# Attention in pairs of steps: four 32-row products side by side, exponential and maximum over two PSUM banks, and one bank for the rotation solver

## The chip, the cores and the metric

One core of one Trainium2 chip. The metric is the device time of one execution in microseconds (us), as the median of several runs; a profiled execution gives the trace from which the rows below are read. The engines are named as the profile names them: PE is TensorE (matmul; PEld its weight loads), DVE is VectorE, ACT is ScalarE, POOL is GpSimd, SP is SyncE.

## The reference

The input is x of shape (2, 512, 144) and a condition vector per batch element. Three transformer layers follow one another, then a learned rotation:

```python
mod = silu(c) @ w_adaln + b_adaln                   # six vectors per batch element
h   = modulate(layernorm(x), shift, scale)
q, k, v = split(h @ w_qkv + b_qkv)                  # 16 heads of 9 columns
attn = softmax(q @ k.T * 9 ** -0.5)                 # 512 x 512 per head and batch element
x = x + gate * (attn @ v @ w_proj + b_proj)
x = x + gate2 * mlp(modulate(layernorm(x), ...))    # layer 0: 4 experts, top 2; layers 1, 2: one MLP of 576
...
R = expm(A(cond))                                   # A skew-symmetric, 64 x 64, one per batch element
```

Layer 1 also normalises each head's q and k. At the end every token is turned in the 64-dimensional subspace that the columns of P span (Q from an orthogonalisation of P, R as above). All is in float32.

## The kernel before

**Blocks, groups, steps.** There are six blocks (three layers by two batch elements). A block has 16 heads in four groups of four. A group has 16 steps (`GSTEPS`), one for each of four tiles of 128 keys and each of four heads `j`. The whole attention is 384 steps, n = 0 to 383. In a step TensorE forms the scores of one key tile and one head against all 512 queries: a product with only 32 rows of contraction (27 used), with `k_t` as weights and `q_t` moving, into one PSUM bank. Head j sits on rows 32j to 32j+31, so products of different heads use different row strips of the array. ScalarE takes the exponential of the bank into `probs` (L667). After every four steps `pv` (L1280) multiplies four heads' `probs` with `v_aug` in eight instructions, each on a strip of 32 columns, into `o_bank`.

**The row maxima.** Softmax needs each query's maximum before the scores of its group. So during group g the kernel also forms, for group g+1, the transposed products (`max_scores`, L1259; 16 per group) in `m_bank`, and VectorE reduces each of them to one column (`take_max`, L823). `MAX_SHARE` puts two of them into each of the first two steps of a group, one into each of the next twelve and none into the last two. In step 14 (`TURN_AT`) `max_turn` (L1267) transposes the maxima with four matmuls, and `place_max` (L830, VectorE) puts them into `q_t`, where they act as one more row of the contraction. The next group's scores wait for that.

**Woven work.** Everything else (adaLN vectors, norms, qkv, projections, gates, MLPs) is cut into slots and spread over the steps by `SLOTS`; it uses two `d_banks`. The solver for the rotation is three chains of small parts spread by `SOLVER_PLAN`: `mgs` and `lu` (64 each, a part every 2.5 steps, up to about step 296), and, from step 141, `skew`, `scale`, eleven `taylor`, `turned` and sixteen `square` (a part every four steps). A solver part is a small TensorE product into PSUM (L1437, L1449, L1460) followed by a chain of small VectorE operations, of which the last (`drain`) releases the bank. The next part of the same chain waits for this release.

**Banks.** Of the eight banks two are for scores, one is `o_bank`, two are for woven work, and three (`m_banks`) form one ring (class `Banks`) that maxima, turns and solver parts take in program order: whoever takes a bank waits until its previous user has drained it. A score product waits for the exponential of two steps before.

**Order on each engine.** Every engine's program is written out by one loop, and each engine runs it in order. TensorE in step n: maxima, scores, the turn of the outputs (`o_turn`), `pv`, `max_turn`, slots, solver parts. VectorE in step n: outputs, slots of step n-1, solver parts of step n-1, then maxima of step n. One of these maxima may be pulled forward (`fill_once`) into the pause of a chain of dependent operations.

```python
            def take(r):
                bk, drained, before = r.take()
                if before:
                    pe.wait_ge(drained, before)
                return bk, (drained, before + 1)
```

## Time and profile before

| | |
|---|---|
| median of 3 runs | 1083.63 us (1082.55 to 1086.33) |
| the profiled execution | 1077.8 us, of which span 1075.7 us |
| mean granted TensorE clock | 0.624 of 2.4 GHz |
| busy: PE, DVE, ACT, POOL | 857.7, 662.4, 385.2, 163.9 us |

The span runs from the first to the last instruction; the rest of an execution's time (2.1 us) lies around it. In rows of the timeline the columns are start in us, duration in us, engine, line, operation, output<-inputs, shapes and count; in brackets stands the idle time just before, with what released the engine. A busy TensorE is not one at its peak: products on different strips run at the same time and count once.

### The profile page before, as it was taken

How to read it: one execution, taken by the hardware profiler on the slowest of the kernel's cores; microseconds unless marked ns; L12 is line 12 of the kernel's file. 1: busy time of each engine (PE TensorE's matmuls, PEld its weight loads, DVE VectorE, ACT ScalarE, POOL GpSimd, SP SyncE). 2: the span in 40 equal slices, each digit the busy share in tenths (PEclk: the TensorE clock that was granted, in tenths of full speed). 3: DMA queues.
4: the chain of work that ended last, by engine and by line, in shares of the span. 5: the costliest groups of instructions: out<-in, count | busy, mean ns of one | idle time of the engine just before them, and what ended most of it. 6: DMA issues, size and time to landing. Idle time of an engine off the chain costs nothing.

```text
span 1075.7 us, 11316 instructions
## 1 busy us (share of the span) xinstructions
PE 857.7 (80%) x3551; PEld 454.5 (42%) x3551; DVE 662.4 (62%) x2080; ACT 385.2 (36%) x682; POOL 163.9 (15%) x353
## 2 busy tenths in 40 slices
PE   5565889896997679799777897979886879979856
PEld 1332333333673333477444343635333544335425
DVE  4478876777537887752578667475767364674232
ACT  0311343332451433345334331325332445545412
POOL 5201013101131000223311003011002021002020
PEclk9855665555796655569865555755555775568557
DMA  3000001000021000002200000000000000000000
GB/s 100 22 1 5 17 12 43 2 16 0 21 64 32 1 0 1 1 16 56 56 0 1 1 1 15 13 1 1 1 1 1 28 1 1 0 1 1 1 11 12
DMA packets 18108, 14.95 MB, mean 14 GB/s; under 512 B 3295, under 2 KB 15479, under 8 KB 18050
## 3 DMA queue, kind: packets, MB, share of 16 engines
q1 hardware_dynamic: 18002, 14.22, 4.8%
q8 instruction: 29, 0.48, 0.2%
q14 instruction: 29, 0.24, 0.1%
q10 hardware_dynamic: 48, 0.02, 0.0%
HBM read 13.62 MB, written 0.61 MB: 13 GB/s over the span
## 4 chain that ended last, share of the span: by engine, by line
PE 61%; DVE 31%; issue 4%; ACT 2%; POOL 2%; DMA 0%; SPq 0%; DVEq 0%; POOLq 0%; ACTq 0%
PE m_bank L1259 11%; PE o_bank L1280 11%; DVE row_max L823 8%; PE d_bank L1399 5%; PE s_bank L1248 3%; PE m_bank L1437 3%; PE d_bank L1341 3%; PE m_bank L1267 2%; PE d_bank L1385 2%; PE d_bank L1230 2%; PE d_bank L1312 2%; DVE h_tok L882 2%; PE d_bank L1386 2%; PE d_bank L1387 2%; PE d_bank L1388 1%
## 5 line engine op out<-in xcount | busy, mean ns | idle before, releaser
L667 ACT ACTIVATE probs<-s_bank 128x512 f32<-128x512 f32 x384 | 220.4, 595 | 486.1 <-PE s_bank L1248 483.5
L823 DVE TENSOR_REDUCE row_max<-m_bank 128x1 fp32r<-128x512 f32 x384 | 256.0, 686 | 151.0 <-PE m_bank L1259 145.8
L1259 PE MATMUL m_bank<-k_t,q_t 32*128 32x512 f32 x384 | 211.8, 731 | 63.1 <-DVE q_rows L1070 24.5
L1248 PE MATMUL s_bank<-q_t,k_t 32*128 32x512 f32 x384 | 233.9, 729 | 6.2 <-ACT probs L667 5.4
L1280 PE MATMUL o_bank<-probs,v_aug 128*32 128x512 f32 x768 | 172.2, 986 | 3.9 <-DVE o_tok L841 3.2
L1259 PEld LDWEIGHTS m_bank<-k_t,q_t 32*128 32x128 f32 x384 | 79.8, 264 | 181.6 <-issue 62.7
L1248 PEld LDWEIGHTS s_bank<-q_t,k_t 32*128 32x128 f32 x384 | 88.2, 265 | 30.6 <-ACT probs L667 15.6
L593 POOL TENSOR_TENSOR h_tok<-h_tok,mod 128x144 f32<-128x144 f32 x48 | 24.0, 500 | 269.2 <-DVE h_tok L882 269.2
L1399 PE MATMUL d_bank<-w_all,g_act 128*128 128x144 f32 x480 | 61.0, 287 | 0.0
L1399 PEld LDWEIGHTS d_bank<-w_all,g_act 128*128 128x128 f32 x480 | 59.4, 190 | 2.3 <-issue 2.3
L1437 PE MATMUL m_bank<-q_rows,ident 64*64 64x144 f32 x128 | 43.9, 442 | 18.9 <-DVE q_rows L1070 18.9
L1312 PE MATMUL d_bank<-ident,h_tok 128*128 128x128 f32 x80 | 32.7, 415 | 19.3 <-POOL h_tok L597 19.3
L1267 PEld LDWEIGHTS m_bank<-ident_r,row_max 128*128 128x128 f32 x96 | 21.5, 312 | 62.2 <-issue 39.2
L596 POOL COPY h_tok<-o_tok 128x144 f32<-128x144 f32 x24 | 7.4, 307 | 257.1 <-DVE o_tok L841 215.4
L733 ACT ACTIVATE g_act<-d_bank 128x512 f32<-128x512 f32 (+1 forms) x60 | 35.7, 597 | 30.0 <-PE d_bank L1388 30.0
L611 POOL TENSOR_TENSOR qs_tok<-qkv_tok,qs_tok 128x144 fp32r<-128x144 f32 x24 | 12.2, 506 | 224.6 <-ACT ks_tok L716 224.6
L1267 PE MATMUL m_bank<-ident_r,row_max 128*128 128x128 f32 x96 | 25.7, 417 | 25.7 <-DVE q_rows L1070 8.7
L1437 PE MATMUL m_bank<-lu,ident 64*64 64x64 f32 x128 | 28.2, 318 | 20.5 <-DVE lu L1092 19.1
L830 DVE SCALAR_TENSOR_TENSOR q_t<-m_bank,q_t 128x512 fp32r<-128x512 f32 x24 | 16.6, 691 | 42.7 <-PE m_bank L1267 42.7
L1437 PEld LDWEIGHTS m_bank<-lu,ident 64*64 64x64 f32 x128 | 17.1, 188 | 54.5 <-DVE lu L1092 26.0
L1437 PEld LDWEIGHTS m_bank<-q_rows,ident 64*64 64x64 f32 x128 | 17.3, 191 | 49.4 <-DVE q_rows L1070 29.5
L1341 PE MATMUL d_bank<-ident_r,qs_tok 128*128 128x128 f32 x96 | 25.1, 410 | 16.2 <-POOL ks_tok L613 16.1
(224 smaller groups left out, 1335.0 us busy)
## 6 DMA issues: line engine op xcount, KB each, us to landing
raw_a<-in_L_cond_w_dram SPq DMA_DIRECT2D x10, 288.0 KB
w_all<-in_L_cond_w_dram SPq DMA_DIRECT2D x10, 288.0 KB
w_rows<-in_L_cond_W_dram SPq DMA_DIRECT2D x8, 141.8 KB
raw_d<-in_L_cond_w_dram SPq DMA_DIRECT2D x30, 36.0 KB
x_tok<-in_x_dram SPq DMA_DIRECT2D x2, 288.0 KB, 4.5
raw_a<-in_L_cond_W_fc_dram SPq DMA_DIRECT2D x2, 288.0 KB
w_all<-in_L_cond_W_fc_dram SPq DMA_DIRECT2D x2, 288.0 KB
out_dram<-moe SPq DMA_DIRECT2D x4, 144.0 KB, 1.9
```

What stands on the lines that cost most here:

```text
L593: link(pool.tensor_tensor(tile, tile, mv[:, first + 1, :], ALU.mult))
L667: act.activation(probs[:, n % PROBS, :], s_banks[n % S_BANKS][:, :], ACT.Exp, scale=HD ** -0.5)\
L733: act.activation(g_act[0:rows, f, :], bk[0:rows, :], ACT.Gelu_apprx_tanh).then_inc(drained, 1)
L823: dve.tensor_reduce(row_max[:, grp % 2, t, MAXROW + 32 * j:MAXROW + 32 * j + 1], bk[:, :], AX.X, ALU.max).then_inc(drained, 1)
L1248: pe.matmul(s_banks[n % S_BANKS][:, :], k_t[rows, par, g, kt * P:(kt + 1) * P], q_t[rows, par, g, :], start=True, stop=True).then_inc(s["s ...
L1259: pe.matmul(bk[:, :], q_t[rows, par, g, t * P:(t + 1) * P], k_t[rows, par, g, :], start=True, stop=True).then_inc(s["max_full"], 1)
L1267: ins = pe.matmul(bk[:, t * P:(t + 1) * P], row_max[:, grp % 2, t, :], ident_r[:, :], start=True, stop=True)
L1280: ins = pe.matmul(o_bank[32 * j:32 * j + 32, :], v_aug[:, par, kt, at:at + 32], probs[:, (GRP * quad + j) % PROBS, :], start=(kt == 0), st ...
L1312: pe.transpose(a_bank[:, cols], h_tok[:, t, 0:P], ident[:, :])
L1341: ins = pe.matmul(bk[:, g * P:(g + 1) * P], src[:, g * GRP:(g + 1) * GRP, :].rearrange("p h w -> p (h w)"), ident_r[:, :], start=True, sto ...
L1399: ins = pe.matmul(dst, g_act[:, f, t * P:(t + 1) * P], w2_all[:, i, f, :], start=(f == 0), stop=(f == FT))
L1437: ins = pe.matmul(bk[0:S, 0:src.shape[1]], ident[0:S, j:j + 1].to_broadcast([S, S]), src, start=True, stop=True)
```

## The change

Two consecutive steps become one pair, 192 in all (`PAIRS`), eight to a group (`GPAIRS`). The score banks become one tensor of two banks, `s_pair`; two of the three maxima banks become `m_pair`; the third, `x_bank`, serves the solver and the turns alone, as a ring of one.

- `scores(p)` issues two products (two heads) into `s_pair` with one signal, and waits for the exponential of pair p-1. ScalarE takes the exponential over both banks with one instruction.
- `max_scores` issues two products into `m_pair` with one signal, after the scores of the pair, and waits until the previous pair of maxima is reduced (`maxed`). VectorE reduces both banks with one instruction, to two columns. For group 0, ahead of the loop, `m_pair` and `s_pair` alternate, and the wait is for the reduction two pairs before.
- `MAX_AT` gives the maxima of a pair the two heads that its scores don't use, so that four strips are in use; one extra pair of maxima comes at the end of pair 1 (after `pv`), and pair 7 has none.
- `max_turn` moves from step 14 to after the scores and `pv` of pair 7, the last. It waits for all the maxima and for `x_bank`.
- `pv` comes in odd pairs, slots and solver parts of both steps come at the end of the pair. Where both steps have a solver part, or a step has two, they follow each other on the one `x_bank`. On VectorE `fill_once` is allowed only while fewer than two such parts are left.

```diff
-S_BANKS, M_BANKS, D_BANKS = 2, 3, 2
+D_BANKS = 2
+PAIR = 2
...
-MAX_SHARE = [2, 2] + [1] * (GSTEPS - 4) + [0, 0]
-TURN_AT = GSTEPS - 2
+MAX_AT = [[(0, 1)], [(1, 0), (0, 0)]] + [[divmod(p + 1, 2)] for p in range(2, GPAIRS - 1)] + [[]]
+TURN_AT = GPAIRS - 1
...
+def slots_of(p):
+    return SLOTS[PAIR * p] + SLOTS[PAIR * p + 1]
+
+
+def parts_of(p):
+    return SOLVER_PLAN[PAIR * p] + SOLVER_PLAN[PAIR * p + 1]
...
-        s_banks = [bank(f"s_bank{i}") for i in range(S_BANKS)]
+        s_pair = ctx.enter_context(nc.psum_tensor("s_pair", [P, PAIR * 512], F32))
+        m_pair = ctx.enter_context(nc.psum_tensor("m_pair", [P, PAIR * 512], F32))
         o_bank = bank("o_bank")
-        m_banks = [bank(f"m_bank{i}") for i in range(M_BANKS)]
+        x_bank = bank("x_bank")
...
-        def ring_m():
-            return Banks(m_banks, m_drained)
+        def ring_x():
+            return Banks([x_bank], [x_drained])
...
-                act.wait_ge(s["scores_full"], n + 1)
-                act.activation(probs[:, n % PROBS, :], s_banks[n % S_BANKS][:, :], ACT.Exp, scale=HD ** -0.5)\
+                act.wait_ge(s["scores_full"], p + 1)
+                act.activation(probs[:, n % PROBS:n % PROBS + PAIR, :],
+                               s_pair[:, :].rearrange("p (i n) -> p i n", i=PAIR), ACT.Exp, scale=HD ** -0.5)\
                     .then_inc(s["probs_ready"], 1)
...
-            def take_max(grp, t, j):
-                bk, drained, _ = mring.take()
+            def take_max(grp, t, half, pair):
                 dve.wait_ge(s["max_full"], seen.next("max_full"))
-                dve.tensor_reduce(row_max[:, grp % 2, t, MAXROW + 32 * j:MAXROW + 32 * j + 1], bk[:, :], AX.X, ALU.max).then_inc(drained, 1)
+                rows = row_max[:, grp % 2, t, :].rearrange("p (j w) -> p j w", j=GRP)
+                dve.tensor_reduce(rows[:, PAIR * half:PAIR * half + PAIR, MAXROW],
+                                  pair[:, :].rearrange("p (i n) -> p i n", i=PAIR), AX.X, ALU.max)\
+                    .then_inc(s["maxed"], 1)
...
-                    taken = [mring.take() if part[0] in SOLVER_BANK else None for part in SOLVER_PLAN[n - 1]]
-                    fill[0] = fill_once
-                    for _ in range(SLOTS[n - 1]):
+                    left = sum(part[0] in SOLVER_BANK for part in parts_of(p - 1))
+                    fill[0] = fill_once if left < 2 else lambda: None
+                    for _ in range(slots_of(p - 1)):
                         next(woven)
...
+                if p:
+                    pe.wait_ge(s["probs_ready"], p)
+                for i in range(PAIR):
+                    rows = slice(32 * (first + i), 32 * (first + i) + 32)
+                    ins = pe.matmul(s_pair[:, 512 * i:512 * i + 512], k_t[rows, par, g, kt * P:(kt + 1) * P],
+                                    q_t[rows, par, g, :], start=True, stop=True)
+                ins.then_inc(s["scores_full"], 1)
...
-                bk, _ = take(mring)
-                pe.matmul(bk[:, :], q_t[rows, par, g, t * P:(t + 1) * P], k_t[rows, par, g, :],
-                          start=True, stop=True).then_inc(s["max_full"], 1)
+                if issued >= depth:
+                    pe.wait_ge(s["maxed"], issued + 1 - depth)
+                for i in range(PAIR):
+                    rows = slice(32 * (PAIR * half + i), 32 * (PAIR * half + i) + 32)
+                    ins = pe.matmul(pair[:, 512 * i:512 * i + 512], q_t[rows, par, g, t * P:(t + 1) * P],
+                                    k_t[rows, par, g, :], start=True, stop=True)
+                ins.then_inc(s["max_full"], 1)
...
-            for n in range(BLOCKS * STEPS):
-                grp = n // GSTEPS
-                if grp + 1 < BLOCKS * G:
-                    for t, j in max_tiles(n):
-                        max_scores(grp + 1, t, j)
-                scores(n)
-                if n % GSTEPS == 4 and grp > 0:
+            for p in range(PAIRS):
+                grp = p // GPAIRS
+                maxima = list(max_pairs(p)) if grp + 1 < BLOCKS * G else []
+                scores(p)
+                for t, half in maxima[:1]:
+                    max_scores(grp + 1, t, half, m_pair, 1)
+                if p % GPAIRS == 2 and grp > 0:
                     o_turn(grp - 1)
-                if n % GRP == 2 and n > GRP:
-                    pv(n // GRP - 1)
-                if n % GSTEPS == TURN_AT and grp + 1 < BLOCKS * G:
+                if p % 2 == 1 and p > 2:
+                    pv(p // 2 - 1)
+                for t, half in maxima[1:]:
+                    max_scores(grp + 1, t, half, m_pair, 1)
+                if p % GPAIRS == TURN_AT and grp + 1 < BLOCKS * G:
                     max_turn(grp + 1)
-                for _ in range(SLOTS[n]):
+                for _ in range(slots_of(p)):
                     next(woven)
-                for part in SOLVER_PLAN[n]:
+                for part in parts_of(p):
                     solver(part)
```

## Rows read from the trace of the kernel before

**Rows 1.** The cores' spans and granted clock, and the page's busy times.

```profile
core 0: 1075.7 us, clock 0.624
...
PE 857.7 (80%) x3551; PEld 454.5 (42%) x3551; DVE 662.4 (62%) x2080; ACT 385.2 (36%) x682; POOL 163.9 (15%) x353
```

**Rows 2.** The page's chain that ended last, by line.

```profile
PE m_bank L1259 11%; PE o_bank L1280 11%; DVE row_max L823 8%; PE d_bank L1399 5%; PE s_bank L1248 3%; PE m_bank L1437 3%; PE d_bank L1341 3%; PE m_bank L1267 2%; PE d_bank L1385 2%; PE d_bank L1230 2%; PE d_bank L1312 2%; DVE h_tok L882 2%; PE d_bank L1386 2%; PE d_bank L1387 2%; PE d_bank L1388 1%
```

**Rows 3.** Groups by line: count | busy, mean ns | idle before and releaser.

```profile
L667 ACT ACTIVATE probs<-s_bank 128x512 f32<-128x512 f32 x384 | 220.4, 595 | 486.1 <-PE s_bank L1248 483.5
L823 DVE TENSOR_REDUCE row_max<-m_bank 128x1 fp32r<-128x512 f32 x384 | 256.0, 686 | 151.0 <-PE m_bank L1259 145.8
...
L936 DVE TENSOR_TENSOR x_tok<-x_tok,gated 128x288 f32<-128x288 f32 x20 | 9.2, 458 | 0.7
...
L1002 DVE TENSOR_TENSOR moe<-moe,mod 128x576 f32<-128x576 f32 x2 | 1.5, 757 | 0.1
```

**Rows 4.** Windows: start:end, length, busy of PE, PEld, DVE, ACT, POOL, clock, DMA.

```profile
194.77:221.15 26.38, 22.76 (x84) 7.99 (x85) 20.40 (x67) 9.61 (x17) 0.00 (x0) 0.50 0.01 1
...
591.96:621.60 29.64, 25.02 (x104) 10.30 (x100) 18.19 (x53) 9.82 (x17) 0.00 (x0) 0.50 0.00 1
...
715.94:759.67 43.73, 40.04 (x174) 23.74 (x171) 24.76 (x68) 20.98 (x43) 4.48 (x8) 0.54 0.00 1
759.67:790.60 30.93, 26.30 (x120) 12.02 (x116) 22.09 (x61) 9.82 (x17) 0.00 (x0) 0.50 0.00 1
...
906.44:926.27 19.83, 19.16 (x76) 6.67 (x72) 11.19 (x19) 9.51 (x17) 0.00 (x0) 0.50 0.00 1
```

**Rows 5.** The same windows, PE instructions that read k_t alone (both products).

```profile
715.94:759.67 43.73, 11.01 (x32) 0.54 0.00 1
...
sum 1075.70, PE 257.98; mean PE 10.32
```

**Rows 6.** Timeline of group 19, from its first scores on.

```profile
908.34 0.79 PE L1248 MATMUL s_bank<-q_t,k_t 32*128 32x512 f32 x1
...
910.60 1.94 PE L1280 MATMUL o_bank<-probs,v_aug 128*32 128x512 f32 x8
912.47 0.28 PEld L1259 LDWEIGHTS m_bank<-k_t,q_t 32*128 32x128 f32 x1 [1.67 <-issue]
...
913.30 1.29 DVE L823 TENSOR_REDUCE row_max<-m_bank 128x1 fp32r<-128x512 f32 x2 [1.79 <-PE m_bank L1259]
913.33 1.08 ACT L667 ACTIVATE probs<-s_bank 128x512 f32<-128x512 f32 x2
...
915.24 1.94 PE L1280 MATMUL o_bank<-probs,v_aug 128*32 128x512 f32 x8
...
918.61 0.28 PEld L1248 LDWEIGHTS s_bank<-q_t,k_t 32*128 32x128 f32 x1 [1.01 <-ACT probs L667]
...
924.41 1.94 PE L1280 MATMUL o_bank<-probs,v_aug 128*32 128x512 f32 x8
926.27 0.93 PEld L1267 LDWEIGHTS m_bank<-ident_r,row_max 128*128 128x128 f32 x4 [1.66 <-issue]
```

**Rows 7.** Timeline: lu parts and what follows them, in groups 11 and 12.

```profile
603.39 0.79 PE L1259 MATMUL m_bank<-k_t,q_t 32*128 32x512 f32 x1
...
604.12 0.69 PE L1449 MATMUL m_bank<-rot,skew_b 64*64 64x64 f32 x4
...
608.23 0.47 PE L1437 MATMUL m_bank<-lu,ident 64*64 64x64 f32 x2
...
608.74 0.15 DVE L1083 TENSOR_SCALAR s_sign<-m_bank 64x1 f32<-64x1 f32 x1 [1.51 <-PE m_bank L1437]
...
623.55 0.15 DVE L1083 TENSOR_SCALAR s_sign<-m_bank 64x1 f32<-64x1 f32 x1
...
624.80 0.29 PEld L1437 LDWEIGHTS m_bank<-lu,ident 64*64 64x64 f32 x2 [0.87 <-DVE lu L1092]
```

**Rows 8.** Timeline of group 17: TensorE held by an lu part.

```profile
866.88 0.44 PE L1437 MATMUL m_bank<-lu,ident 64*64 64x64 f32 x2 [5.23 <-DVE lu L1092]
```

More of the change, by code:

```diff
@@ L739, in solver @@
                 if step[0] in SOLVER_BANK:
-                    bk, drained, before = mring.take()
+                    bk, drained, before = xring.take()
                     full = seen.next("solver_full")
@@ L1167, in solve @@
             def solve(part):
-                solver(part, mring.take() if part[0] in SOLVER_BANK else None)
+                solver(part, xring.take() if part[0] in SOLVER_BANK else None)
             for slot, _ in enumerate(side(HEAD)):
@@ L1172, in _ @@
                     solve(part)
[L1173 to L1175 removed]
+            for i in range(HALVES * T):
+                take_max(0, *divmod(i, HALVES), (m_pair, s_pair)[i % 2])
+                for part in first_parts(2 * i + 1):
                     solve(part)
```

119 lines of the change are left out of this document (56 added, 63 removed).

## The prediction

> **What bounds the kernel now.** I read the cores row first: a span of 1075.7 us at a mean granted clock of 0.624, so TensorE runs mostly at the lower of its two levels [rows 1]. The busy times name it as the fullest engine (857.7 us), VectorE next (662.4) [rows 1]. The chain by line shows that no single line bounds the time: the two kinds of 32-row products hold 14% of it, `pv` 11%, the reductions 8%, and the rest is woven work and solver parts in small shares [rows 2]. ScalarE idles 486 us before its exponentials [rows 3], so they cost nothing by their number. What counts is the order in which the in-order TensorE meets the answers of the others. So I cut the span at each turn of the maxima (L1267) into 24 windows; window k holds group k. Those without slots are short: 19.8 us without a solver (group 19), 26.4 with `mgs` (3), 29.6 with `lu` and `taylor` (11), 30.9 with `lu` and `square` (15); with six slots and a solver 43.7 (14) [rows 4]. I walk the new order through these kinds with the durations of the trace, and multiply.
>
> **Part 1, products side by side.** Products on different strips already start together: at 912.47 four of them, for two steps, are over when the first output turn begins [rows 6]. A batch with a switch of shape before and after it takes 603.39 to 604.12, so 0.73 us, at the low clock [rows 7]. Before, one step's two products make such a batch wherever a slot, a solver part or `pv` comes between two steps; after, only every pair does. TensorE is busy with these products for 258.0 us in all, 10.3 per window, 11.0 in group 14 [rows 5]. After: eight batches of 0.79 and one more of 0.43 for the extra maxima of pair 1, which use the same strips as the scores of pair 2: 6.8 us. The upper bound of the gain is 3.5 us per window. Groups with slots, where TensorE has no other reason to stop, get most of it at the low clock and about half of it at the high one. Over the 15 groups with many slots (0 to 2, 4 to 6, 8 to 10, 12 to 14, 16 to 18) I take 3.0 us in the seven that also hold solver parts of two chains (8 to 10, 12 to 14, 16), and 1.75 in the other eight, of which some wait for VectorE anyway: -21 and -14, together -35 us.
>
> **Part 2, one instruction over two banks.** The trace has none. Bounds for VectorE: two reductions in a row take 1.29 us [rows 6], so no more than that; from 288 to 576 columns an operation grows by 299 ns, 1.04 ns per column [rows 3], so 686 + 512 x 1.04 ns = 1.22. I take 1.22: 0.07 less per pair, 13 us of VectorE in all, of which perhaps a tenth is on the path (8% of the chain is this line [rows 2]): -1 us, mostly ahead of the loop, where eight rounds are paced by VectorE. For the exponentials 1.08 (two in a row [rows 6]) is the upper end; I take 1.05. The Trainium skill (Advanced Engine Details and Errata, in its part on the SBUF/PSUM latency) advises just this, several PSUM banks read by one instruction, since the latency is exposed between instructions; the 0.07 us is what this trace leaves for it, because neighbours already overlap.
>
> **Part 3, the buffers are one deep.** Scores of pair p wait for the exponential of p-1. From the issue of a batch to the start of its exponential 0.86 us pass (912.47 to 913.33), of its reduction 0.83 (to 913.30) [rows 6]; the release costs 0.05. So scores can follow each other every 0.86 + 1.05 + 0.05 = 1.96 us, and maxima every 0.83 + 1.22 + 0.05 = 2.10, at the low clock. From one `pv`'s end (912.47) to the next `pv` 2.77 us pass now with an output turn between (to 915.24) [rows 6]; after: 2.10 + 0.73 = 2.83. Equal. Two places differ. First, pair 1: after its `pv` come the extra maxima; those of pair 2 wait 2.10 us for them, with the output turn queued behind, and those of pair 3 again 2.10 for those. Group 19, from its first scores at 908.34: `pv` starts at 2.83 (now 2.26), its end is 4.7; maxima of pair 2 at 6.8, output turn 7.5 to 8.6, maxima of pair 3 at 8.9, second `pv` at 9.6 (now 6.9), third at 14.3, last at 18.8 (now 16.07, 924.41), its end is 20.6 (now 17.93, 926.27) [rows 6]. That is +2.7 us. The turn and the placing (908.34 - 906.44 = 1.9) stay. I book 2.7 for 19, 2.3 for 20 (half at the high clock), 2 for 21 to 23 together (some slots; the last has no maxima): +7. Beside this walk a rule of the Trainium skill (Perfetto Trace Analysis, Optimizing Tensor Performance, Matmuls) asks that independent products rotate through banks, so that one is emptied while the next is filled; the change takes this rotation away, and the walk is what it costs by the rows.
>
> **Part 4, the solver on one bank.** In 24 pairs two solver parts follow each other (one in each of groups 2, 8 and 16, two in 9, three in 10, 11, 13, 14 and 15, four in 12: so many by `parts_of`). Before, `taylor` or `square` went out right behind `lu` into another bank. Now it waits until `lu` is drained: 0.51 us from its issue to VectorE's first operation (608.23 to 608.74), 1.25 from there to the next product that waited for the chain (623.55 to 624.80), less the 0.40 that `lu` itself takes: 1.4 us [rows 7]. Behind it in TensorE's queue stand the next pair's scores, and ScalarE waits for those. That is the lower bound, with VectorE idle; the upper is a VectorE in the midst of a norm, which now holds TensorE 5.23 us at one `lu` [rows 8]. For the 17 in groups with slots I take 1.75: +30 us.
>
> Group 11 pair by pair, with each `lu`'s chain stretched by the reduction put into its pause (1.13): pair 0 5.45 us (products, 2.2 for the previous group's `lu`, which now stands behind the turn, `lu`, 1.4, `taylor` 0.7), pair 1 3.0, pair 2 6.4, pair 3 3.0, pair 4 5.5, pair 5 3.0, pair 6 3.55, pair 7 with turn, placing and its `lu` 4.85: 34.7 against 29.6 [rows 4], +5. Group 15 the same way, with `square`'s eight products (1.1): 37.4 against 30.9 [rows 4], +6.5. Together +11.5.
>
> Groups 3 and 7 have one part per pair, of 2.2 us on VectorE without and 2.9 with the reduction, at distances of two, two, two and four steps in place of two and three: 1.9 + 4.2 + 4.4 + 3.7 + 3.7 + 2.6 + 1.9 + 5.1 = 27.5 against 26.4 [rows 4]: +1.1 each, +2. In the eight slot groups of part 1 without a second chain the same crowding and the part that now stands behind the placing (0.4 to 0.7) make +7.
>
> **The sum.** -35 - 1 + 7 + 30 + 11.5 + 2 + 7 = +21.5 us on the profiled execution's 1077.8, so 1099.3. The median of the runs shown is 1083.63, 5.8 above that execution; I put the change on the median: 1105 us. POOL, SP and the DMAs lose nothing: their loops only drop counting. A measurement of this kernel can't tell less than 0.3% (3 us) from no change.
>
> **Rivals.** *The wait is only moved (faster).* TensorE waits for the solver today as well: 5.23 us at one `lu` [rows 8], 0.87 at another [rows 7]. If the wait at the second part only takes the place of one that came a batch or two later, the 24 pairs cost nothing: -30, and -1.4 x 6 in groups 11 and 15. Sum: 21.5 - 38.5 = -17, so 1067. The point that decides: with these pairs free the sum is -17, so they tip it when they cost 17 us, 0.73 each over the 23 that I booked. For it: such waits are in most solver groups. Against: group 11 has only 4.6 us of TensorE idle to give [rows 4], and the clock is low there either way.
>
> *VectorE falls behind (slower still).* TensorE may now lead VectorE by one pair of maxima and one solver part, where three banks let it lead by more. If each of the 20 norms costs 1.5 us more of the kind of the 5.23 [rows 8], the time is 1105 + 30 = 1135. For it: VectorE is busy 24.8 of 43.7 us in group 14 and idle in bits [rows 4]. Against: in those stretches it was VectorE's chain that set the pace already.
>
> *No effect.* Gain and loss cancel: 1081 to 1087.
>
> **How the numbers follow.** The forecast case, 1090 to 1122 (each of the two large terms off by half), 0.50; the wait only moved 0.25; VectorE behind 0.19; no effect 0.06. The likeliest is 1105. The range from 1070 to 1136 leaves out part of the first rival and the far end of the second. Faster 0.25, same 0.06, slower 0.69.
>
> **What the new profile would show.** Right: TensorE's busy time for these products near 258 - 23 x 3.5 = 178 us; the exponential near 1.05 and the reduction near 1.22 us; new idle of TensorE before L1449 and L1460 put down to `lu`; a group 19 of 22.5 us and a group 11 of 34 to 35. Wrong: idle before `taylor` and `square` small, a group 11 under 31 us, or slot groups shorter by more than 3.5 us each, which would mean that a batch costs more around itself than 0.73 us.

## The result: slower by 49 us, and the profile after

The changed kernel takes 1132.98 us (median of four runs, 1131.26 to 1135.42) beside 1084.02 us for the kernel before (four runs, 1082.55 to 1086.33): a ratio of 1.045, 95% interval 1.042 to 1.048. The forecast was slower, 1105 us. The direction was right and the time lies inside the range given, but the rise is 49 us where the sum had 21.5. The profiled execution is 55.4 us longer in span than the one before. Single executions of the kernel before lie between 1066 and 1091 us, with medians of 1084 to 1086; where they fall into shorter and longer ones, a ratio given with an interval compares the shorter ones alone.

The page of the kernel after, busy time by engine (to be set beside [rows 1]) and the chain by line (beside [rows 2]):

```profile
PE 799.3 (71%) x3551; PEld 435.4 (38%) x3551; DVE 655.5 (58%) x1888; ACT 361.1 (32%) x490; POOL 163.5 (14%) x353
...
PE 54%; DVE 34%; ACT 5%; issue 5%; POOL 2%; DMA 0%; DVEq 0%; SPq 0%; ACTq 0%; POOLq 0%
PE o_bank L1300 11%; DVE row_max L833 10%; PE s_pair L1264 9%; PE d_bank L1419 5%; PE x_bank L1457 4%; PE d_bank L1361 3%; PE m_pair L1279 3%; ACT probs L680 2%; PE x_bank L1287 2%; PE d_bank L1244 2%; PE d_bank L1405 2%; DVE h_tok L894 2%; PE x_bank L1480 1%; DVE q_rows L1082 1%; PE d_bank L1247 1%
```

TensorE lost 58 us of busy time, as it was meant to, and the kernel became longer. So TensorE's idle time grew from 1075.7 - 857.7 = 218.0 us to 1131.1 - 799.3 = 331.8: by 114. The rest of this text asks what the 114 are.

Groups by line (columns as in [rows 3]: busy and mean ns, then idle before with its releaser):

```profile
L680 ACT ACTIVATE probs<-s_pair 128x1024 f32<-128x1024 f32 x192 | 196.3, 1022 | 510.7 <-PE s_pair L1264 510.3
L833 DVE TENSOR_REDUCE row_max<-m_pair 128x2 fp32r<-128x1024 f32 x188 | 229.9, 1223 | 108.6 <-PE m_pair L1279 106.6
...
L1264 PE MATMUL s_pair<-q_t,k_t 32*128 32x512 f32 x384 | 142.2, 737 | 28.1 <-ACT probs L680 21.5
```

The two new instructions take 1022 and 1223 ns. The exponential's idle time before it grew from 486 to 511 us: ScalarE is not the engine that is short.

The waits of TensorE (engine, what waited, for what; us in total, times, longest):

```profile
PE x_bank L1457 <- DVE q_rows L1082: 63.1, 31, 6.3
PE x_bank L1457 <- DVE lu L1104: 44.6, 20, 6.6
PE x_bank L1480 <- DVE lu L1104: 31.9, 15, 5.8
PE x_bank L1469 <- DVE lu L1104: 30.3, 10, 7.3
PE s_pair L1264 <- ACT probs L680: 21.5, 21, 2.2
```

L1457 is the product of a `mgs` or `lu` part, L1480 that of `square`, L1469 that of `taylor`. These four solver rows hold 170 us of idle. The second two, 62.2 us in 25 waits, are the ones that the prediction named: a part of the second chain behind `lu`. The same waits before, and with them those of the maxima, which shared the ring with the solver:

```profile
PE m_bank L1437 <- DVE lu L1092: 19.1, 10, 5.5
PE m_bank L1437 <- DVE q_rows L1070: 18.9, 19, 2.4
PE m_bank L1449 <- DVE lu L1092: 5.0, 3, 3.7
PE m_bank L1460 <- DVE lu L1092: 2.3, 2, 1.2
PE m_bank L1259 <- DVE q_rows L1070: 24.5, 11, 7.1
PE m_bank L1259 <- DVE lu L1092: 16.9, 12, 4.1
```

They are 45.3 us for the solver's own products and 41.4 for the maxima, 86.7 in all. So 83 of the 114 us stand in front of solver products now. Where the waiting stands is not yet its cause; that takes the experiments.

The windows of groups 3, 11, 14, 15 and 19 (columns as in [rows 4], which has the same groups of before), and under them the products that read `k_t` in group 14 and in all windows (beside [rows 5]):

```profile
198.45:226.19 27.74, 21.40 (x84) 7.29 (x85) 19.79 (x59) 8.78 (x9) 0.00 (x0) 0.50 0.01 1
613.56:647.62 34.06, 22.06 (x104) 9.12 (x100) 17.69 (x45) 8.78 (x9) 0.00 (x0) 0.50 0.00 1
754.45:803.41 48.96, 36.82 (x175) 22.92 (x171) 24.19 (x60) 20.09 (x35) 4.02 (x8) 0.53 0.00 1
803.41:838.76 35.35, 24.42 (x121) 11.07 (x117) 21.55 (x53) 8.78 (x9) 0.00 (x0) 0.50 0.00 0
956.63:979.85 23.22, 18.43 (x77) 6.31 (x73) 10.97 (x11) 8.78 (x9) 0.00 (x0) 0.50 0.00 1
...
754.45:803.41 48.96, 6.90 (x32) 0.53 0.00 1
...
sum 1131.10, PE 183.84; mean PE 7.35
```

Group 14 is the plain case. Its products fell from 11.0 to 6.9 us, its TensorE time from 40.0 to 36.8, and it takes 49.0 us in place of 43.7. All of the difference is TensorE standing still: 3.7 us before, 12.1 after.

Cut at the turns of the maxima as in the prediction, and put into its classes, the 24 groups and the head (time up to the first turn) differ by:

| groups | forecast, us | measured, us |
|---|---|---|
| 8 to 10, 12 to 14, 16: slots and two chains | -21 + 30 = +9 | +37.6 |
| 0 to 2, 4 to 6, 17, 18: slots, at most one chain or few doubled pairs | -14 + 7 = -7 | +0.6 |
| 11 and 15 | +11.5 | +8.8 |
| 3 and 7 | +2 | +1.4 |
| 19 and 20 | +5 | +7.7 |
| 21 to 23 | +2 | -2.5 |
| head | -1 | +1.7 |

The miss has one place: the seven groups with slots and two chains hold 28.6 of the 34 us between the profiled difference and the sum. There the pair kernel stands like this (timeline in group 12, all engines; in brackets the idle time before an instruction):

```profile
682.67 1.02 ACT L680 ACTIVATE probs<-s_pair 128x1024 f32<-128x1024 f32 x1 [5.66 <-PE s_pair L1264]
...
684.72 0.94 DVE L875 BATCH_NORM_STATS2 stat<-x_tok 128x6 f32<-128x144 f32 x4
...
684.83 0.44 PE L1457 MATMUL x_bank<-lu,ident 64*64 64x64 f32 x2 [2.25 <-DVE lu L1104]
...
688.29 1.62 DVE L894 TENSOR_SCALAR h_tok<-x_tok,mean_var,rstd 128x144 f32<-128x144 f32 x4
...
689.83 0.14 DVE L1095 TENSOR_SCALAR s_sign<-x_bank 64x1 f32<-64x1 f32 x1
...
690.67 0.28 DVE L1104 SCALAR_TENSOR_TENSOR lu<-x_bank,s_small,lu 64x64 f32<-64x64 f32 x1
...
691.00 1.11 PE L1480 MATMUL x_bank<-rot 64*64 64x64 f32 x8 [5.73 <-DVE lu L1104]
...
692.88 1.02 ACT L680 ACTIVATE probs<-s_pair 128x1024 f32<-128x1024 f32 x1 [9.19 <-PE s_pair L1264]
```

TensorE issues the `lu` product at 684.83. VectorE is in a norm (L875 to L894) until it turns to the bank at 689.83, and it drains the bank only at 690.95. The `square` product needs that same bank, so TensorE stands for 5.73 us; the next scores are behind it in the queue, and ScalarE has nothing for 9.19 us. This is the prediction's upper case, at one place. The doubled pair in group 11, where VectorE is free, is its lower case:

```profile
618.96 0.44 PE L1457 MATMUL x_bank<-lu,ident 64*64 64x64 f32 x2 [2.08 <-DVE lu L1104]
619.51 0.15 DVE L1095 TENSOR_SCALAR s_sign<-x_bank 64x1 f32<-64x1 f32 x1 [0.70 <-PE x_bank L1457]
...
620.36 0.28 DVE L1104 SCALAR_TENSOR_TENSOR lu<-x_bank,s_small,lu 64x64 f32<-64x64 f32 x1
620.70 0.69 PE L1469 MATMUL x_bank<-rot,skew_b 64*64 64x64 f32 x4 [1.30 <-DVE lu L1104]
```

1.30 us, where the walk had 1.4. If seventeen such pairs were the cause of the 28.6 us, each would have to cost 1.75 + 1.7 = 3.4 us. That was the first theory to test.

### The profile page after: what moved, and what is told of

Read it like the earlier page. It is cut to its first block, busy times and chain, and to the rows that moved or that the text cites. A ratio compares the mean times of both kernels' runs of the same rounds, so it can differ in the third digit from the quotient of the medians.

```text
span 1131.1 us, 10906 instructions
## 1 busy us (share of the span) xinstructions
PE 799.3 (71%) x3551; PEld 435.4 (38%) x3551; DVE 655.5 (58%) x1888; ACT 361.1 (32%) x490; POOL 163.5 (14%) x353
## 4 chain that ended last, share of the span: by engine, by line
PE 54%; DVE 34%; ACT 5%; issue 5%; POOL 2%; DMA 0%; DVEq 0%; SPq 0%; ACTq 0%; POOLq 0%
PE o_bank L1300 11%; DVE row_max L833 10%; PE s_pair L1264 9%; PE d_bank L1419 5%; PE x_bank L1457 4%; PE d_bank L1361 3%; PE m_pair L1279 3%; ACT probs L680 2%; PE x_bank L1287 2%; PE d_bank L1244 2%; PE d_bank L1405 2%; DVE h_tok L894 2%; PE x_bank L1480 1%; DVE q_rows L1082 1%; PE d_bank L1247 1%
## 5 line engine op out<-in xcount | busy, mean ns | idle before, releaser
L680 ACT ACTIVATE probs<-s_pair 128x1024 f32<-128x1024 f32 x192 | 196.3, 1022 | 510.7 <-PE s_pair L1264 510.3
L833 DVE TENSOR_REDUCE row_max<-m_pair 128x2 fp32r<-128x1024 f32 x188 | 229.9, 1223 | 108.6 <-PE m_pair L1279 106.6
L1264 PE MATMUL s_pair<-q_t,k_t 32*128 32x512 f32 x384 | 142.2, 737 | 28.1 <-ACT probs L680 21.5
L1279 PE MATMUL m_pair<-k_t,q_t 32*128 32x512 f32 x376 | 140.6, 744 | 10.8 <-DVE row_max L833 10.2
L1457 PE MATMUL x_bank<-q_rows,ident 64*64 64x144 f32 x128 | 44.4, 446 | 68.6 <-DVE q_rows L1082 63.1
L1264 PEld LDWEIGHTS s_pair<-q_t,k_t 32*128 32x128 f32 x384 | 52.0, 267 | 94.2 <-ACT probs L680 53.9
L1279 PEld LDWEIGHTS m_pair<-k_t,q_t 32*128 32x128 f32 x376 | 50.9, 266 | 57.2 <-DVE row_max L833 54.9
L1457 PE MATMUL x_bank<-lu,ident 64*64 64x64 f32 x128 | 27.6, 313 | 54.9 <-DVE lu L1104 44.6
L1457 PEld LDWEIGHTS x_bank<-q_rows,ident 64*64 64x64 f32 x128 | 17.6, 194 | 96.0 <-DVE q_rows L1082 82.6
L1457 PEld LDWEIGHTS x_bank<-lu,ident 64*64 64x64 f32 x128 | 16.9, 186 | 83.2 <-DVE lu L1104 54.5
L747 ACT ACTIVATE g_act<-d_bank 128x512 f32<-128x512 f32 (+1 forms) x60 | 35.3, 595 | 32.0 <-PE d_bank L1408 31.5
L1287 PEld LDWEIGHTS x_bank<-ident_r,row_max 128*128 128x128 f32 x96 | 21.8, 316 | 51.4 <-issue 48.3
L1405 PE MATMUL d_bank<-h_hi,ff_hi 128*128 128x512 f32 x60 | 30.9, 515 | 12.7 <-ACT g_act L747 7.7
```

The costliest lines, as they stand in the source:

```text
L680: act.activation(probs[:, n % PROBS:n % PROBS + PAIR, :], s_pair[:, :].rearrange("p (i n) -> p i n", i=PAIR), ACT.Exp, scale=HD ** -0.5)\
L747: act.activation(g_act[0:rows, f, :], bk[0:rows, :], ACT.Gelu_apprx_tanh).then_inc(drained, 1)
L833: dve.tensor_reduce(rows[:, PAIR * half:PAIR * half + PAIR, MAXROW], pair[:, :].rearrange("p (i n) -> p i n", i=PAIR), AX.X, ALU.max)\
L1264: ins = pe.matmul(s_pair[:, 512 * i:512 * i + 512], k_t[rows, par, g, kt * P:(kt + 1) * P], q_t[rows, par, g, :], start=True, stop=True)
L1279: ins = pe.matmul(pair[:, 512 * i:512 * i + 512], q_t[rows, par, g, t * P:(t + 1) * P], k_t[rows, par, g, :], start=True, stop=True)
L1287: ins = pe.matmul(bk[:, t * P:(t + 1) * P], row_max[:, grp % 2, t, :], ident_r[:, :], start=True, stop=True)
```

## The experiments

The theory at the start (**solver**): the doubled pairs on one bank cost far more than 1.75 us. The rival (**order**): they cost what was booked, and it is the -35 us of the products side by side that doesn't come, since TensorE meets other waits with the time saved. Given the spread of single executions, differences under some 10 us between two variants carry little. The recorded expectations name runs by label: e4, e5 and e6 are 3, 4 and 5 here, e12 and e13 are 9 and 10, e14 and e15 are 16 and 17, e17 is 11. Their theory A is the solver theory, their rivals B and C are crowding of the solver's parts and the one-deep buffers.

**1 and 2. Without the second chain, in pairs and in steps.** The same edit in both kernels:

```diff
-EXP_CHAIN = [("skew",), ("scale",)] + [("taylor", n) for n in range(TAYLOR - 1, 0, -1)] + [("turned",)]
-EXP_CHAIN += [("square", i) for i in range(SQUARINGS)]
+EXP_CHAIN = [("skew",), ("scale",), ("turned",)]
...
-                    pe.wait_ge(*last[chain])
+                    pe.wait_ge(s["rot_ready"], 1)
```

> The pair kernel without the 11 taylor and 16 square parts (the matrix exponential is left out, so the rotation is not the reference's). This leaves 2 pairs with two parts for the one bank in place of 24. Theory A, one bank: TensorE's idle before the second parts (30.3 us before taylor, 31.9 before square) goes, and with it 22 us of small products: 1133 to about 1050, and less than 1.5% above the kernel before with the same parts left out. Rival B, crowding and one-deep buffers everywhere: only the parts' own work goes, some 25 us, and the pair kernel stays 40 us behind the kernel before with the same parts left out.

> The kernel before without the 11 taylor and 16 square parts (the matrix exponential is left out). It gives what these parts cost where they have banks to themselves: both theories say 20 to 30 us, so about 1058. The distance to the pair kernel without them is the test: under 15 us by theory A, about 40 us by rival B.

Measured: 1060.56 us in pairs (1055.57 to 1064.38) and 1042.55 in steps (1031.23 to 1044.81): pairs are 18 us slower where only two pairs are doubled (one in group 2, one in group 8), 49 with the chain. In the seven groups of the miss the difference is +13.5 us (320.8 against 307.3) without the second chain and +37.6 with it. So the 16 doubled pairs that go from these groups cost 24.1 us, 1.5 each: less than the 1.75 booked. The rest is a +13.5 that stands where the sum had -21. One caution: the profiled execution in steps is the shortest of its four (1031.23), so the two profiles differ by 33 us where the medians differ by 18. Even if all of these 15 us stood in the seven groups, the difference there would be near nothing, and not -21. For the whole kernel the second chain's extra price in pairs is 22 us by the profiles and 31 by the medians, for 22 pairs: 1.0 to 1.4 each. The solver theory fails for the miss; it holds for what was booked.

**3. The extra maxima taken away.** A pair of maxima in every pair of steps, none extra, on the strips that the scores leave free:

```diff
-MAX_AT = [[(0, 1)], [(1, 0), (0, 0)]] + [[divmod(p + 1, 2)] for p in range(2, GPAIRS - 1)] + [[]]
+MAX_AT = [[(p // 2, 1 - p % 2)] for p in range(GPAIRS)]
```

> The pair kernel with one pair of maxima in each of the eight pairs of a group, pair 7 too, and no extra one behind pair 1. The walk of the prediction puts the loss of a group without slots on the extra maxima (the maxima of pairs 2 and 3 wait 2.1 us each): if so, groups 19 and 20 get 2 to 2.5 us shorter, the four or five other light groups 1 us, and the whole 8 to 15 us. Rival: in group 19 the time goes to the one-deep score pair; then nothing moves by more than 3 us.

Measured: 1110.25 us (1107.75 to 1111.72), 23 less, where 8 to 15 were expected. Group 19 falls from 23.22 us to 18.36:

```profile
943.02:961.38 18.36, 14.57 (x76) 5.65 (x73) 10.97 (x11) 8.79 (x9) 0.00 (x0) 0.76 0.00 1
```

The granted clock is 0.76 in that window and was 0.50 before, so not all of the 4.9 us is the order: the later run 15, the same order on one bank but with its parts elsewhere, has 21.33 at 0.50 in group 19. The extra maxima are a cost that the prediction booked at +7; about three times that came back. By the windows of the two profiles, 9.5 of the 23 us stand in groups 19 to 23 and 13.6 in the groups before them.

**4. The ring of three kept.** Maxima one by one in the ring of three banks that the solver and the turns share, as before; scores and exponential stay in pairs:

```diff
-        m_pair = ctx.enter_context(nc.psum_tensor("m_pair", [P, PAIR * 512], F32))
-        x_bank = bank("x_bank")
+        m_banks = [bank(f"m_bank{i}") for i in range(3)]
...
+                    bk, _ = take(xring)
+                    pe.matmul(bk[:, :], q_t[rows, par, g, t * P:(t + 1) * P],
+                              k_t[rows, par, g, :], start=True, stop=True).then_inc(s["max_full"], 1)
```

> Only the scores and exponentials in pairs; the maxima one bank and one reduction at a time, in one ring of three banks with turns and solver parts as in the kernel before, in the pair kernel's order. Theory A: the second parts get another bank, so their 60 us of waits mostly go, and most of the products still start together: 1075 to 1095. Rival B: the solver parts at the end of every pair, one pair apart, and the one-deep scores are what costs: it stays above 1110.

Measured: 1086.11 us (1083.31 to 1088.20), 47 less than the changed kernel and equal to before. TensorE is as little busy (799.8 us): the time is idle that went away, 331.8 to 282.5 us. Nearly all of the loss goes when the maxima and the solver have their ring back, and yet the paired scores then gain nothing.

**5. Scores released one bank at a time.** Two exponentials, each on its own bank of `s_pair`, and each score product waits for the one on its bank:

```diff
+                for i in range(PAIR):
+                    act.wait_ge(s["scores_full"], n + i + 1)
+                    act.activation(probs[:, (n + i) % PROBS, :], s_pair[:, 512 * i:512 * i + 512],
+                                   ACT.Exp, scale=HD ** -0.5).then_inc(s["probs_ready"], 1)
```

> The pair kernel with the scores of a pair as two steps again: each product waits for its own bank, signals by itself, and has its own exponential (384 of 0.6 us in place of 192 of 1.02). It takes away what is one deep on the score side. TensorE's idle before the scores that is put down to the exponential is 21.5 us. Theory A: that is a small part, 1123 to 1133. Rival B (one-deep scores are a main cause): under 1115.

Measured: 1132.29 us (1125.27 to 1139.91), beside 1132.98 for the changed kernel. No gain. The one-deep score buffer is not what holds the full kernel.

**6. The two parts of a doubled pair apart.** The first goes between the maxima and `pv` of its own pair, so that products and `pv` lie between the two:

```diff
+def early_parts(p):
+    parts = parts_of(p)
+    return parts[:1] if sum(part[0] in SOLVER_BANK for part in parts) == 2 else []
```

> The pair kernel, but where a pair has two parts for the one bank, the first goes out right behind the pair's first products (before output turn, pv and slots), on VectorE too, and the second stays at the end. Nothing else changes. Theory A: TensorE's waits before taylor and square (62 us in all) fall under 20 us; 35 to 50 us of the 49 lost come back: 1085 to 1100. Rival B, crowding of the solver: the waits move to the next part, before L1457, and the time stays above 1115.

Measured: 1122.49 us (1120.00 to 1122.63), 10.5 less. The waits of TensorE:

```profile
PE x_bank L1475 <- DVE lu L1117: 68.6, 25, 7.6
PE x_bank L1475 <- DVE q_rows L1095: 64.6, 31, 6.4
...
PE x_bank L1498 <- DVE lu L1117: 15.0, 12, 2.3
```

L1475 is L1457 of the changed kernel, L1498 is L1480. The waits of `square` and `taylor` fell from 62 to 26 us, and those of the `lu` product rose from 44.6 to 68.6. Two thirds of what was taken away came back one part later. With one bank and two chains the wait travels.

**7 and 8. Parts further apart.** One `mgs` or `lu` part every three steps in place of two and a half (`QR_PACE` 6 for 5), in pairs and in steps.

```diff
-QR_PACE = 5
+QR_PACE = 6
```

> The pair kernel with a part of the mgs/lu chain every three steps in place of every 2.5 (QR_PACE 6), so that two of three pairs hold one, and the chain reaches into the last block. TensorE is idle 123 us before these parts. If crowding of this chain is a second cause, as theory C says, this gives 20 to 30 us back in the pair kernel, and much less in the kernel before. Under theory A alone it gives under 10 us here (the number of doubled pairs falls from 24 to about 20).

> The kernel before with the mgs/lu chain every three steps (QR_PACE 6). Theory C: its parts are two or three steps apart already and TensorE runs ahead past them, so 0 to 8 us less. If it gains as much as the pair kernel does, crowding is no cost of the change.

Measured: 1110.53 us in pairs (1108.38 to 1113.55), 1098.86 in steps (1090.55 to 1103.54). Pairs gain 22, steps lose 15, where 0 to 8 less was expected. The gap between them shrinks from 49 to 12 us. For both the chain now reaches into groups 19 to 22, which take 19.5 us more in steps and 11.0 more in pairs. For pairs the better spacing outweighs that: their seven groups with two chains become 13.0 us shorter.

**9 and 10. Almost no solver.** Of the first chain only 15 `mgs` parts and one `lu` remain, moved to the end, and the second chain is left out as in 1; in pairs and in steps:

```diff
+QR_CHAIN = [("p_load",)] + [("mgs", j) for j in range(15)] + [("unit_cols",)]
+QR_CHAIN += [("lu", 0)] + [("signs",), ("less_one",), ("y",), ("m", 0), ("m", 1)]
...
+        plan[280 + i * QR_PACE // 2].append(part)
```

> The pair kernel with nearly no solver behind the head: all mgs parts after the 15 ahead of the loop, all lu parts but one, and all taylor and square parts are left out (the rotation is not the reference's); the few others come at step 280 and later. Theory: the 58 us of TensorE time that the side-by-side products save did not shorten the kernel because TensorE spends them before solver parts (its idle before L1457 rose from 39 to 124 us). Then without the parts the pairs win: at least 15 us less than the step kernel cut in the same way. Rival: the saving is lost to the one-deep buffers or to the other engines, and the pair kernel is level with it or behind.

> The kernel before with the same parts left out. What the solver costs in steps: its TensorE products take 95 us of busy time in the whole kernel before, the waits around them some 100; both theories say 920 to 990 us. The distance to the pair kernel cut in the same way is the test.

Measured: 950.33 us in pairs (933.79 to 957.96) and 900.93 in steps (889.05 to 914.21). Both spread widely: with the shorter two executions of each alone (934 and 946, 889 and 898) the distance is 46 us, by the two profiled ones 31.5. The steps came out below the 920 to 990 expected. The theory that the solver eats the saving falls with this: pairs are 46 to 49 us behind without it as well. The first line is group 11 in pairs, the second in steps (windows, columns as above):

```profile
517.12:540.35 23.23, 18.44 (x77) 6.32 (x73) 10.97 (x11) 8.78 (x9) 0.00 (x0) 0.50 0.00 1
```

```profile
495.31:515.14 19.83, 19.15 (x76) 6.67 (x73) 11.19 (x19) 9.50 (x17) 0.00 (x0) 0.50 0.00 1
```

In steps TensorE is idle for 0.7 of 19.8 us, in pairs for 4.8 of 23.2. The pair kernel saves 0.7 us of TensorE in such a group and spends 4.1 on standing. A solver chain can hide this: group 7 takes 28.27 us in the changed kernel and 28.21 in the kernel before, both with `mgs` parts, but 23.22 and 19.83 here, all four at a clock of 0.50. In the changed kernel 6.6 of TensorE's 7.1 idle us in that group stand before solver products, in the kernel before it is idle 3.9. That the chain sets the pace in both and so covers the 3.4 us is what these rows suggest; no run isolates it. Over groups 3, 7, 11, 15 and 19 pairs are 18.8 us behind, of which some 3 are the clock of group 3 in steps (16.87 us at 0.69, where the others have 19.83 at 0.50). TensorE's largest wait in 9 is that of the scores for the exponential, far above the same wait in 10 (first pairs, then steps):

```profile
PE s_pair L1263 <- ACT probs L679: 52.2, 51, 2.4
```

```profile
PE s_bank L1247 <- ACT probs L666: 13.8, 30, 0.9
```

**11 and 12. Even maxima, and scores singly, with almost no solver.** The edits of 3 and 5, each on 9.

> The pair kernel without most solver parts (as e12) and with one pair of maxima in each pair of steps. If the extra pair of maxima in pair 1 is what puts the pairs 49 us behind the steps, this comes to 900 to 915, level with e13. If the one-deep buffers as such do it, it stays above 930.

> The pair kernel without most solver parts and with the scores one by one as in e6. TensorE is idle 52 us before scores, put down to the exponential, in e12. If the one-deep score pair costs time of its own, 20 us or more come back (under 930); if it only stands where the extra maxima would wait anyway, 940 to 950.

Measured: 927.75 us (919.75 to 929.79) and 953.35 (950.64 to 955.44). Against the median of 9 even maxima give back 22 us, against its shorter two executions 12; single release gives nothing, although the waits of scores for the exponential are the largest in 9 (52.2 us, 30.2 with single release). The distance to steps is 27 us by the medians. The profiled executions can't say in which groups it stands, since they differ by only 5.5 us (919.75 is the shortest of 11, 914.21 the longest of 10). But the light groups can be set side by side at one clock: at 0.50, group 19 takes 19.83 us in 10, 23.22 in 9 and 21.33 in 11.

**13 and 14. Half exponentials.** The exponential reads half of each bank's columns, in 11 and in 10; the other half of `probs` holds ones, so the attention's values are left out in part.

```diff
-                act.activation(probs[:, n % PROBS:n % PROBS + PAIR, :],
-                               s_pair[:, :].rearrange("p (i n) -> p i n", i=PAIR), ACT.Exp, scale=HD ** -0.5)\
+                act.activation(probs[:, n % PROBS:n % PROBS + PAIR, 0:256],
+                               s_pair[:, :].rearrange("p (i n) -> p i n", i=PAIR)[:, :, 0:256], ACT.Exp, scale=HD ** -0.5)\
```

> e17 (pairs, few solver parts, even maxima) with the exponential over the first 256 of the 512 queries alone (the other half is left out and holds a constant), so 0.6 in place of 1.02 us per pair. In every even pair TensorE is idle 1.17 us until the exponential is done. If these waits (51.6 us in all, put down to the exponential) are what is left of the loss, up to 0.4 us in some 96 pairs comes back and the time falls from 928 by 20 to 40 us, to 888 to 908. If something else takes over (the maxima at 2.1 us are next), by less than 10.

> e13 (steps, few solver parts) with the same half of the exponentials left out, 0.33 in place of 0.6 us each. TensorE's idle put down to the exponential is 13.8 us there: 0 to 12 us less than 901. The distance between the two is the test.

Measured: 919.24 us in pairs (917.40 to 921.87), 9 less; 875.80 in steps (868.84 to 893.73), 25 less, where 0 to 12 were expected. Part of the 25 is the clock, 0.714 in the profiled execution against 0.658 in that of 10. If pairs were held by the one-deep exponential, they would have gained more than steps. They gained less, and the gap grew to 43. That theory falls too, and group 19 shows it at one clock: in steps it goes from 19.83 to 18.87 us, in pairs it stays where it was (the window in 11, then in 13):

```profile
752.41:773.74 21.33, 17.37 (x76) 5.91 (x72) 10.97 (x11) 8.78 (x9) 0.00 (x0) 0.50 0.00 0
```

```profile
751.14:772.47 21.33, 18.45 (x76) 6.20 (x72) 10.97 (x11) 5.37 (x9) 0.00 (x0) 0.50 0.00 0
```

The trace of 13 shows what holds it. Two pairs of steps and a `pv` form a round:

```profile
767.73 0.79 PE L1279 MATMUL m_pair<-k_t,q_t 32*128 32x512 f32 x2
...
768.60 1.23 DVE L833 TENSOR_REDUCE row_max<-m_pair 128x2 fp32r<-128x1024 f32 x1 [1.41 <-PE m_pair L1279]
...
769.88 0.28 PEld L1279 LDWEIGHTS m_pair<-k_t,q_t 32*128 32x128 f32 x2 [0.33 <-DVE row_max L833]
...
770.61 1.93 PE L1300 MATMUL o_bank<-probs,v_aug 128*32 128x512 f32 x8
```

The second maxima of the round wait until the first are reduced, some 2.15 us after the issue of the first, and `pv` stands behind them in the queue. The second scores of the round come 1.54 us after the first in 13 and 1.97 in 11, but its second maxima come after some 2.15 in both, and from one `pv` to the next it is 4.75 us in both. In a light group with even maxima the pace is set by the one-deep `m_pair`.

**15. Even maxima, parts by step, one bank.** The edit of 3, and the parts of the first step of a pair go right behind the pair's products, those of the second to its end:

```diff
+def early_parts(p):
+    return SOLVER_PLAN[PAIR * p]
+
+
+def late_parts(p):
+    return parts_of(p)[len(early_parts(p)):]
```

> The pair kernel with its single solver bank and its maxima in m_pair, even maxima (e4), and the parts of a pair's first step behind the pair's products (as e15). Against e4's 1110: if the place of the parts is the cause, it gains as e15 did over e14, to 1075 to 1085. If the ring of three is what counts, it stays above 1095.

Measured: 1082.07 us (ten runs, 1080.71 to 1091.81), ratio 1.000 (0.996 to 1.003): 28 less than with even maxima alone. The whole loss is gone with the single bank still there.

**16 to 18. The ring of three with it.** First the ring of 4 with the maxima of 3; then with the parts of 15 as well; last that kernel with the single release of 5.

> Ring of three (e5) and one pair of maxima in each pair of steps (e4) together. If the two savings of 47 and 23 us have different places they add up in part: 1062 to 1075, faster than the kernel before by 1% or more. If both took away the same wait, it stays at 1080 to 1088.

> As e14, but the solver parts of a pair's first step go out right behind the pair's products (before output turn, pv and slots) and on VectorE right behind its maxima; those of the second step stay at the end. The parts of the mgs/lu chain then come at distances near the 2.5 steps of the kernel before. If crowding at the pair's end is what eats the saving, 10 to 25 us less than e14. If not, within 5 us of it.

> e15 with the scores one by one. TensorE is idle 26 us before scores in e15, put down to the exponential. If these waits bind, 5 to 15 us less than e15; if the products then start less often four at a time, the same or more.

Measured: 1088.21 us (1083.70 to 1091.96), 1056.28 (1053.66 to 1059.18) and 1069.24 (1065.15 to 1071.64). The middle one has a ratio of 0.984 (0.972 to 0.995) to the kernel before: by the medians it is 28 us shorter, by the ratio 17. It is 77 us shorter than the changed kernel. It came out lower than expected (32 us less than 16, not 10 to 25); the last came out 13 us longer than 17 in place of 5 to 15 shorter. In 16 the two savings were expected to add up in part, and even maxima alone add nothing to the ring. TensorE's maxima behind `lu`, in 16 and then in 17:

```profile
PE m_bank L1277 <- DVE lu L1103: 63.8, 24, 7.5
```

```profile
PE m_bank L1295 <- DVE lu L1118: 37.4, 13, 7.5
```

In experiment 4 this wait was 38.9 us. So with even maxima and the solver parts still bunched at the end of the pair, the maxima more often find the ring held by `lu`. Spreading the parts does not simply free it: in 17 the maxima wait 28.3 us for the reduction as well (6.1 in 16), 65.7 us by both against 69.9. What falls are the waits of the `mgs` and `lu` products for their own chains, from 85.7 us to 38.4.

## Why the prediction was right in direction and short in size

**The products side by side (-35 us): the step that failed.** What it says of TensorE's time was right: these products went from 258.0 to 183.8 us where 178 were forecast. What failed is that it put the new waits behind them at nothing: it turned 3.0 us of busy time in a group with slots and two chains into 3.0 us of span, -21 over the seven. Measured, those groups are 13.5 us longer even with no second chain and 1.8 us longer with almost no solver and even maxima (each by its profiled executions, which scatter as said at runs 1 and 11). In none of the three comparisons of pairs with steps (full, without the second chain, almost no solver) are these seven groups shorter in pairs. A batch that ends sooner lets TensorE arrive sooner at the next wait: in run 9 against run 10 TensorE is busy 46.6 us less and idle 78.2 us more (some of the busy time is the clock, 0.706 against 0.658). The table is of the profiled executions.

| kernel | TensorE busy, us | idle, us |
|---|---|---|
| before | 857.7 | 218.0 |
| after | 799.3 | 331.8 |
| 3: even maxima | 768.2 | 339.8 |
| 15: and parts by step | 774.7 | 315.3 |
| 17: and ring of three | 773.5 | 283.6 |
| 10: steps, few parts | 739.6 | 172.8 |
| 9: pairs, few parts | 693.0 | 251.0 |

**The one bank at doubled pairs (+30 and +11.5): right in kind, somewhat high.** 1.30 us in group 11 for 1.4; 24 us for 16 of the 17 pairs, for which 28 of the 30 were booked; groups 11 and 15 +8.8 for +11.5, with the walks of group 11 34.7 (measured 34.06) and of 15 37.4 (35.35). The true price lies near the lower of the two bounds, 1.4 and 5.23. By the prediction's own count 18 doubled pairs stand in groups with slots; the one in group 2 is in no term, which at 1.75 us changes nothing.

**The light groups and the extra maxima (+7): the walk right, its reach too small.** Group 19 measured 23.22 us, forecast 22.5. In the timeline the scores of group 19 start at 958.53, `pv` at 961.86, the extra maxima at 963.72, those of pair 2 after the reduction:

```profile
963.72 0.79 PE L1279 MATMUL m_pair<-k_t,q_t 32*128 32x512 f32 x2
...
965.84 0.80 PE L1279 MATMUL m_pair<-k_t,q_t 32*128 32x512 f32 x2 [0.90 <-DVE row_max L833]
```

That is 2.12 us for the 2.10 of the walk. Its first `pv` comes late, 3.33 us after the first scores where the walk had 2.83: the maxima of pair 1, ahead of it in the queue, already wait for the reduction of those of pair 0. In the kernel before this stretch took 2.26 us (908.34 to 910.60), and it stays at 3.33 with even maxima and with half the exponential (runs 11 and 13): of the 1.5 us by which group 19 stays behind in these runs, 1.1 are here. But the order costs in all groups, not in those without a solver alone: taking the extra maxima away gave 23 us in the full kernel and 12 to 22 in the one with few parts. The prediction charged them to groups 19 to 23 and let the others off. The advice of the Trainium skill beside this walk (Perfetto Trace Analysis, Optimizing Tensor Performance, Matmuls: independent products should rotate through banks) points the right way for maxima and solver: the ring of three brought 47 us in run 4 and 26 us between runs 15 and 17, and group 19 at 0.50 goes from 21.33 us with even maxima on one pair to 20.33 with them on the ring (run 16). Giving the scores their rotation back did nothing in runs 5 and 12 and cost 13 us in run 18.

**One instruction over two banks (-1): right.** 1223 ns against 1.22 us, 1022 against 1.05. The gain of that size is lost in the rest.

**Crowding in groups with one chain (+2, +7).** Groups 3 and 7 +1.4; the eight slot groups +0.6 where -14 + 7 were expected. The two terms can't be told apart here; if the crowding cost its 7, about half of the -14 came.

**The rivals.** *The wait is only moved* has something true: in run 6 it did move when taken away. But with all but two of the doubled pairs gone (run 1 against run 2) the pair kernel was 18 us slower, not 17 us faster, so it fell with the same -35. *VectorE falls behind* gave the time best, 1135, by a mechanism that occurs (5.73 us at 691.00) but isn't shown to be the bulk: the second chain's extra price was 22 to 31 us, and VectorE is busy 58% of the span. No run isolates the share of the norms. *No effect* fell.

**What the loss is made of.** By runs in the full kernel, one edit after another: 1133 us; extra maxima away, 1110; parts by step, 1082; ring of three, 1056. Steps of 23, 28 and 26 us, each larger than the change's whole gain was forecast to be in any class. They don't simply add in another order: even maxima on the ring brought nothing until the parts were spread.

**What stays open.** With almost no solver and even maxima the pairs still lie 27 us behind the steps (927.75 against 900.93). It is not the single release of the score banks and not the exponential's length. In a light group the trace of run 13 names the one-deep `m_pair`, which is 1.5 us in group 19; how much it is in the groups with slots no run shows, since the kernel with few parts was not run with even maxima on the ring. Nor was the kernel before run with even maxima, so how much of the 17 to 28 us by which run 17 beats it comes from the fusing is not shown. A second bank for the second chain alone, taken from the `d_banks`, was not tried.

## What to carry to other kernels

Time saved on the fullest engine is worth its waits: before booking it, take each stage and ask what the engine meets next in its queue and whether that will be ready sooner. Here 74 us of products vanished and 114 us of idle came. When steps are fused, keep what lay between them: spread the parts of a dependent chain over the fused step, keep extra batches out, and give each kind of short-lived product more than one bank; those three were worth 77 us here, and only with all three was a kernel of fused steps shorter than the kernel before (1056 us against 1084). And price a wait by removing its cause in both kernels: an experiment in the new kernel alone (1133 to 1061 without the second chain) would have blamed the solver for 72 us, of which 42 belong to it in the old kernel as well.

## What the runs showed of the chip that was not expected

- An exponential over two banks takes 1022 ns, where two in a row took 1.08 us [rows 6] and one alone 595 ns [rows 3]: joining saves 0.06 us. The reduction saves 0.07 of 1.29. Two in a row already took less than twice the time of one, so joining them saved next to nothing.
- The same light group can come at different granted clocks from kernel to kernel. Group 20 with even maxima, in run 16 and then in run 17:

```profile
936.60:956.21 19.61, 15.73 (x81) 5.35 (x77) 11.47 (x19) 8.79 (x9) 1.90 (x8) 0.56 0.00 0
```

```profile
920.15:935.27 15.12, 9.92 (x77) 3.52 (x77) 11.38 (x19) 8.79 (x9) 1.90 (x8) 1.00 0.00 0
```

  One is at 0.56 of full speed, the other at 1.00, and 4.5 us lie between them. The stretch ahead differs too: group 19 has 0.50 in the first and 0.75 in the second. Some of every difference between two variants is of this kind, and a difference read in one group alone should be read beside its clock.
